# A decoder of two layers: alternating scan steps, and B's rows spread through device memory

## The reference

```python
xs, res = split(rmsnorm(x) @ W_in);  xs = silu(depthwise_causal_conv(xs))
xdbc = xs @ W_xp;  dt_r, B, C = xdbc[:, :128], xdbc[:, 128:144], xdbc[:, 144:160]
delta = softplus(dt_r @ W_dt + b_dt)                     # [256 tokens, 512 channels]
h[t] = exp(delta[t] * A) * h[t-1] + delta[t] * B[t] * u[t]   # 512 channels x 16 states
y = sum over states of h[t] * C[t];   y = (y + u * D) * silu(res);  out = y @ W_out + x
...
y = einsum(silu(g) * u, w_down) for 16 experts, weighted by routing, plus a shared expert
```

## Time and profile before

| | |
|---|---|
| three runs, us | 983.55, 986.10, 978.01 (median 983.55) |
| the profiled execution: its own time, and its span | 984.03 and 982.2 us |
| busy share of the span | PE 89%, DVE 65%, ACT 39%, POOL 37% |
| TensorE's mean granted clock | 0.955 of full |
| first scan step of sequences 0, 1, 2, 3 starts at | 112.6, 315.8, 535.2, 759.5 us |

### The profile page before, as it was taken

One profiled execution on the slowest core, in us unless ns is written; L12 is line 12 of the kernel. 1 busy time (PEld: TensorE's weight loads), 2 busy tenths in 40 slices (PEclk: granted clock), 3 DMA queues, 4 the chain that ended last, 5 costly groups with the idle time before them and its releaser, 6 DMA issues.

```text
span 982.2 us, 13012 instructions
## 1 busy us (share of the span) xinstructions
PE 870.8 (89%) x4643; PEld 652.0 (66%) x4668; DVE 643.3 (65%) x1378; ACT 383.9 (39%) x828; POOL 358.9 (37%) x393
## 2 busy tenths in 40 slices
PE   6897675988999998889999998888999998789997
PEld 5675344754787786744787886653788786426886
DVE  6332799795355998895355999875355999764333
ACT  4111743326236443426326443417226544243111
POOL 5202485120042875220043875220042876000322
PEclk9897877999999999999999999979999999879999
DMA  6204000002023330301024330302022330300452
GB/s 217 110 0 175 0 1 0 1 14 98 1 81 113 126 113 2 107 29 82 1 81 145 97 111 1 108 1 110 1 68 69 94 109 17 108 1 1 129 153 84
DMA packets 22196, 67.69 MB, mean 69 GB/s; under 512 B 2860, under 2 KB 4780, under 8 KB 21492
## 3 DMA queue, kind: packets, MB, share of 16 engines
q1 hardware_dynamic: 21876, 66.80, 20.8%
q10 hardware_dynamic: 256, 0.07, 0.0%
HBM read 65.74 MB, written 1.05 MB: 68 GB/s over the span
## 4 chain that ended last, share of the span: by engine, by line
PE 49%; DVE 19%; POOL 12%; issue 12%; ACT 7%; DMA 1%; ACTq 1%; POOLq 0%; DVEq 0%; SPq 0%
PE B L779 22%; PE F L779 21%; POOL arena L465 7%; DVE arena L1430 5%; DVE nmx L1501 3%; PE B L1068 3%; POOL spare L550 2%; ACT big L746 2%; POOL arena L475 2%; PE F L808 1%; DVE arena L1270 1%; DVE arena L1442 1%; PE F L790 1%; POOL rs L447 1%; PE B L1149 1%
## 5 line engine op out<-in xcount | busy, mean ns | idle before, releaser
L779 PE MATMUL B<-spare,mw 128*128 128x256 f32 x880 | 209.3, 382 | 0.0
L779 PEld LDWEIGHTS B<-spare,mw 128*128 128x128 f32 x880 | 166.5, 191 | 24.8 <-issue 2.6
L550 POOL TENSOR_TENSOR spare<-q_t 128x256 f32<-128x256 f32 x112 | 82.0, 738 | 193.3 <-DVE q_t L1567 134.2
L1430 DVE TENSOR_TENSOR_SCAN arena<-F,arena 128x512 f32<-128x512 f32 x128 | 149.5, 1207 | 3.7 <-ACT F L702 2.3
L465 POOL TENSOR_TENSOR arena<-du,arena 128x1024 f32<-128x1024 f32 x60 | 140.9, 2360 | 9.8 <-PE F L779 8.5
L702 ACT ACTIVATE F<-delta,a_neg 128x255 f32<-128x255 f32 x256 | 109.9, 467 | 72.6 <-DVE arena L1430 72.6
L779 PE MATMUL B<-mw,spare 128*128 128x256 f32 x448 | 115.4, 381 | 1.2 <-POOL spare L550 1.2
L779 PE MATMUL F<-arena,ident 128*128 128x256 f32 x400 | 105.1, 406 | 1.4 <-POOL arena L475 1.0
L768 ACT ACTIVATE q_t<-B 128x256 f32<-128x256 f32 x112 | 42.0, 381 | 159.2 <-PE B L779 152.6
L1562 DVE SCALAR_TENSOR_TENSOR q_t<-q_t,B 128x256 f32<-128x256 f32 x112 | 46.6, 416 | 77.7 <-ACT q_t L768 77.4
L779 PEld LDWEIGHTS B<-mw,spare 128*128 128x128 f32 x448 | 84.2, 190 | 15.9 <-POOL spare L550 3.9
(11 more groups left out here) (228 smaller groups left out, 1284.0 us busy)
## 6 DMA issues: line engine op xcount, KB each, us to landing
mw<-in_w_moe SPq DMA_DIRECT2D x112, 384.0 KB, 3.1
room<-in_w_f SPq DMA_DIRECT2D x4, 2544.0 KB, 9.1
room<-in_w_l SPq DMA_DIRECT2D x4, 768.0 KB, 7.1
w_m<-in_w_m SPq DMA_DIRECT2D x1, 2112.0 KB
room<-in_w_l SPq DMA_DIRECT2D x4, 512.0 KB, 4.9
x_t<-in_x_t SPq DMA_DIRECT2D x4, 256.0 KB, 3.3
x_tok<-in_x_tok SPq DMA_DIRECT2D x4, 256.0 KB, 6.4
y<-x SPq DMA_DIRECT2D x4, 256.0 KB, 2.2
```

Of the source, the lines that this page charges most:

```text
L550: g.tensor_tensor(hid1[0:r, m % HID_RING, :], hraw[0:r, m % 3, :], crs[0:r, int(m >= MTE), :], ALU.mult)\
L779: return t_.matmul(dst, lhsT, rhs, start=start, stop=stop, skip_group_check=True)
L1430: v.tensor_tensor_scan(h, F[i][:, :], h, 0.0, ALU.mult, ALU.add)\
```

## The change

**Scan order.** Step n is now state pair k = n // 2 of channel pair n % 2. The two pairs alternate, so C's pair is spread once for two steps, eight times for a sequence. Each channel pair sums into a bank of its own, the first into F[3], the second into K[2]. Both are gated in u1, and step 9 gates nothing.

**B.** PE and ACT no longer spread B. SP writes the 16 rows of B (16 KB) to a scratch in device memory, waits for it, and then issues eight transfers that read a pair of rows (2 KB) into all 128 partitions of b_rep, 256 KB each. POOL waits for these.

**The experts.** K[2] is taken, so while a front runs beside the back the tiles go through K[0] and K[1] (gate_bank), and PE's tile m waits for DVE's tile m-2 where it waited for m-3. The last back, which runs alone, keeps three banks. SP's request for the weights of tile m+6 stands three phases later in its own order, with the same wait.

**Order.** All four tables are new.

```diff
+        def gate_bank(b, m):
+            return K[m % (3 if b == B - 1 else 2)]
+        def y_bank(dp):
+            return K[2] if dp else F[3]
...
+                if ph == "d1":
+                    sp.wait_ge(*af.at("bct", b))
+                    sp.dma_start(b_out[b], bct[0:NS, :]).then_inc(b_saved, 16)
+                    sp.wait_ge(b_saved, b * 16 + 16)
+                    for k in range(NK):
+                        sp.dma_start(b_rep[:, k, :], b_out[b, 2 * k:2 * k + 2, :].rearrange("s t -> (s t)")
+                                     .partition_broadcast(P)).then_inc(rep_in[k], 16)
...
-                if ph in BE and BE.index(ph) + MW_RING < MT1:
-                    m = BE.index(ph)
+                if ph in BE and 3 <= BE.index(ph) < MT1 - MW_RING + 3:
+                    m = BE.index(ph) - 3
                     sp.wait_ge(*pb.at(f"down{m}", b))
...
-                dp, k = divmod(n, NK)
+                k, dp = divmod(n, 2)
                 if dp == 0:
-                    pool.wait_ge(*af.at(f"rep{k}", b))
+                    pool.wait_ge(rep_in[k], b * 16 + 16)
...
-                if ph == "d3":
-                    replicate(b, 0)
...
-                    for k in (1, 2, 3):
-                        replicate(b, k)
...
-                spread(F[2], NS + 2 * (n % NK), f"c{n}")
+                spread(F[2], NS + n, f"c{n}")
...
-                        last = mm(F[3][:, i * S:i * S + S], ident[:, :], state(n)[:, i, s * S:s * S + S],
+                        last = mm(y_bank(dp)[:, i * S:i * S + S], ident[:, :], state(n)[:, i, s * S:s * S + S],
...
                     n = STEPS.index(ph)
-                    spread_c(b, n)
-                    if n < 2:
-                        for k in (4 + 2 * n, 5 + 2 * n):
-                            replicate(b, k)
+                    if n % 2 == 0:
+                        spread_c(b, n)
...
-                    if m >= 3:
-                        pe.wait_ge(*db.at(f"gu{m - 3}", b))
+                    r = 3 if b == B - 1 else 2
+                    if m >= r:
+                        pe.wait_ge(*db.at(f"gu{m - r}", b))
...
-                    if n == NK + 1:
-                        gated_output(b, 0)
-                    dve.wait_ge(*pf.at(f"c{n}", b))
+                    dve.wait_ge(*pf.at(f"c{n - n % 2}", b))
...
                 if ph == "u1":
+                    gated_output(b, 0)
                     gated_output(b, 1)
...
-AFTER_PE = {"load": 2, "qkv": 1, "at2": 2, "at3": 1, "at4": 2, "at5": 2, "at6": 1, "at7": 7, "oa": 2, "ob": 5, "xa":
-            1, "xb": 1, "xc": 1, "xd": 6, "fa1": 1, "fa2": 1, "fa3": 1, "fg0": 1, "fg1": 1, "fg4": 1, "fg5": 1, "fd1":
-            3, "fd2": 1, "fd3": 2, "m1": 1, "m2": 2, "m3": 1, "d1": 1, "d2": 1, "d3": 1, "d4": 1, "s0": 1, "s1": 1,
-            "s2": 1, "s3": 1, "s4": 1, "s5": 2, "s6": 1, "s7": 2, "s9": 3, "s10": 1, "s11": 1, "s13": 1}
+AFTER_PE = {"load": 2, "qkv": 1, "at1": 1, "at2": 2, "at3": 1, "at4": 2, "at5": 1, "at6": 2, "at7": 3, "oa": 2, "ob":
+            8, "xa": 1, "xb": 1, "xc": 4, "xd": 3, "fa1": 1, "fa2": 1, "fa3": 2, "fg0": 1, "fg2": 1, "fg3": 3, "fd1":
+            1, "fd2": 1, "m1": 4, "m2": 1, "m3": 1, "d3": 1, "d4": 1, "s0": 3, "s3": 1, "s4": 5, "s6": 1, "s7": 1,
+            "s8": 3, "s10": 1, "s11": 2, "s13": 1}
```

74 lines of the change are left out of this document (29 added, 45 removed), and 6 rows, old and new, of the table AFTER_DVE.

## The result

The changed kernel takes **969.47 us** (median of four runs, 968.47 to 971.54), against 980.92 for the kernel before in the same comparison: 0.987 of its time, with a 95% interval of 0.984 to 0.990. Its profiled execution took 970.11 us with a span of 968.3, against 984.03 and 982.2. So there are 13.9 us between the two traces, and the prediction's sum had 12.6.

A forecast was written before the change was run, and what follows sets the result against it. The scan was taken as bound by DVE, with PE close behind. Three rounds of -3.3 - 0.6 + 0.2 (scan's end) - 0.3 = -4.0, plus sequence 0's -0.6, made 984.0 - 12.6 = 971.4, said as 971 us; range 962 to 986.

The forecast's parts named there:

- The chain to the first scan: From the copy of B and C to a round's first scan: -3.3 us a round, bounds -3.4 to -0.5.
- The memory's branch: Ahead of the first scan: B written to device memory and read back, 2.2 + 3.1 us, first product done at 312.0 to 312.2.
- ACT's branch: Ahead of the first scan: softplus, table load, tanh and decays on ACT, giving a first scan at 312.4, 3.4 us earlier.
- rival 1: Ahead of the first scan: write and read take 8 us or more, gain 0.5 not 3.3; about 976 to 984, chance 0.26.
- So I count it at nothing: In the scan: 5.8 us a round of PE's spreads removed, valued at nothing by itself because DVE's 70 us hides it.
- The scan stage, -0.6: In the scan: gating leaving step 9 -1.6, new DVE waits +2.2, present waits gone -1.2, so -0.6 us a round.
- The three new waits: In the scan: DVE waits for tile 16 (0.8 us), C's pair in s6 (0.7) and tile 21 (0.7).
- rival 2: Expert tiles in the scan: two banks make DVE wait, 0.5 us a tile, 8.5 a round; above 984, chance 0.11.
- The rest of the round, -0.3 a round: Outside chain and scan: new tables let shifts take up some idle PE time, -0.3 us a round, bounds -2 and +2.
- rival 3: Row maxima ahead of the scan: TensorE's clock fall in sequence 3 (4.8 us) does not come; below 966, chance 0.16.
- Sequence 0, -0.6: Sequence 0's front: scan starts +1.0 us later waiting for memory, gating leaves (-1.6), 0.2 added behind: -0.6 us.
- a risk for the output projection: Sequence 0's front: with less PE work, last sums and output projection may start at the low clock; one fall adds up to 4.8 us.

The follow-up runs named there:

- experiment 4: Changed kernel, with SP writing B's rows to the scratch four times, each waited for, before the reads: 992.1 us, 1.012.
- experiment 1: Kernel before, with only the order of the scan's front changed (five table places moved from behind d1 or d2 to behind s0): 984.12 us, 1.001.
- experiment 3: Changed kernel, but B spread by PE and copied by ACT again, with no scratch in memory: 974.46 us, 0.992.
- experiment 6: Changed kernel, with two of B's eight reads issued at once and six behind the weights of tiles 12 and 13: 966.48 us, 0.983.
- experiment 7: Changed kernel, with each spread of C's pair made three times, 32 more bf16 matmuls a round in the scan: 973.44 us, 0.991.
- experiment 12: The changed kernel again, unaltered, timed in six more runs: 968.57 us, 0.986.
- experiment 8: Changed kernel, with PE making the scores of row maxima 4 to 15 twice ahead of the scan: 982.29 us, 1.000.
- experiment 9: Changed kernel, with the old table order ahead of the scan's front (load to m5), new tables from d1 on: 982.54 us, 0.999.
- experiment 11: Changed kernel with B's reads in two parts and one PE table entry moved, leaving the instruction order the same as without that move: 966.72 us, 0.982.
- experiment 5: Kernel before, with only two banks for the expert tiles beside a front, PE's tile m waiting for DVE's m-2: 992.1 us, 1.010.
- experiment 10: Kernel before, code unchanged, with the new table order only ahead of the scan's front (load to m5): 979.59 us, 0.996.
- experiment 2: Changed kernel's code with the four tables of the kernel before: 991.9 us, 1.012.

## Why the prediction was right, and where it was not

The total, 971 for 969.5, is right, and its largest term is right for the reasons given. The rest holds luck. Between the two traces the scan stages came out 5.6 us worse than forecast over the three rounds; the rest of the rounds (1.8 better), sequence 0 (1.6), the tail (3.2) and the chains (0.3) made up for that. Of these the tail is outside the sum altogether, and the rest of the rounds gained by a clock that the sum had kept out.

**The chain to the first scan: right.** -3.4 measured for -3.3, 7.23 us after the copy for 7.2. The memory's branch took 4.9 us from the write's issue to POOL's start, for 5.3: the write landed in 1.4 where 2.2 was taken, and a read of 256 KB, in a row of eight, has a median of 5.3 on the page:

```profile
arena<-b_out SPq DMA_DIRECT2D x32, 256.0 KB, 5.3
```

That median is of all eight, which share the engines; the first one is what POOL waits for. It is ACT's branch that the forecast called last, and in the trace it ends within 0.1 us of DVE's own products for tile 10, which wait for ACT's tanh. Experiment 4 shows the other side of it: late by 4.3, the memory's branch is last, as rival 1 said. The Trainium skill's figure ("DMA: Bandwidth & Descriptors", "Anatomy of one DMA"), about 2.0 us of fixed cost for a transfer, is fitted to transfers that GpSimd issues; this write, issued by SyncE, took 1.4 us.

**"So I count it at nothing": the step that failed.** The prediction called the scan bound by DVE, with PE close behind, and gave the spreads removed from PE no value. For the order before, the traces bear out the first half: DVE has 69.0 us of work in 73.7, some 2.7 us in gaps of under 0.15 us between its instructions, and only these waits:

```profile
DVE arena L1442 <- PE F L779: 1.3, 3, 0.6
DVE arena L1430 <- POOL arena L458: 0.4, 1, 0.4
DVE q_t L1562 <- ACT q_t L768: 0.2, 1, 0.2
```

But the same change also moves an expert tile from the chain into the stage, and there PE's work is no longer free. Without the removal of work the chain's gain of 4.1 us is given back in full, most of it in DVE's waits for PE (experiment 1). Putting work back on PE in the new order has a price in both runs that do it: 1.1 us a round for B's spreads (experiment 3 against 6), and 1.8 us for twice the spreads of C that the change took away (experiment 7 against 6, at full clock; 1.3 by the medians). An estimate from these, 1.1 and half of 1.8, is that the removed spreads are worth about 2 us a round. With all of the change and the weights in time (experiment 6) the stage is 4.3 us shorter than in experiment 1; what else is in this, with DVE's 2.3 us less of work the nearest, isn't shown. The size of the work was off as well: 48 matmuls by 8.7 us made 0.18 each. In the changed kernel's trace a pair from 309.89 on is busy for 0.38 us, yet the next matmul starts at 310.11, 0.22 us after it, and one more in a row costs 0.105 (experiment 7), so 32 fewer are 3.4 us of PE a round and not 5.8.

DVE's work went from 69.0 to 67.5 us, and little of that is seen: even in experiment 6 the stage is only 0.3 us shorter than before. DVE's waits are 2.6 us there where they were 1.9.

**The scan stage, -0.6: it was +0.9, +1.8 and +1.1.** The prediction's walk followed DVE, counted 1.6 for the gating that leaves, and called tile 12's late weights covered because DVE takes the tile only near 325. The lateness itself was forecast well (a request at 308.5, PE waiting some 2 us), and a wait of that size is covered: where no half clock follows it the stage is 73.5 (experiment 12). The three new waits that the walk found for DVE are there as well, 0.8, 1.0 and 0.8 us for 0.8, 0.7 and 0.7. What was missed is the half clock that mostly follows, and that on PE the next spread of C stands behind tiles 12 and 13, so DVE meets the delay at 322 and not at 325. In 18 stages (the changed kernel's two traces, experiments 6, 8, 9 and 11) the length is 73.4 us and this one wait of DVE, to within 0.15 us. It is 1.30, 2.15 and 1.51 us in the changed kernel, not there in experiments 6 and 11, and up to 3.40 in experiment 8. So this is 1.2 to 2.0 us a round. Without it the term would have been -0.3, near the forecast.

**Two banks, rival 2.** The mechanism exists: 8.6 us in the old order (experiment 5), just as the rival priced it for one round, over three. In the changed kernel the stage shows no PE wait for a DVE product, as the walk had found; in experiment 6 there is one of 1.6 us, whose cost was not measured. So the new tables hide the two banks in the changed kernel; whether they do once the weights are in time is open.

**The rest of the round, -0.3 a round.** The new order ahead of the scan gives the first two rounds nothing (+0.4 and +1.3 after, +1.1 and +0.2 in experiment 10), and the third 3.7. There the half clock of 10.2 us doesn't come. That is part of rival 3, which the prediction priced at 4.8 and kept out of its sum. It is in experiment 10, where nothing else is changed, and in its median, -4.5.

The rival's reason is not borne out, though. It had the new order prevent the fall of the clock. In the traces with that order (the changed kernel twice, experiments 3, 4, 6, 7, 8, 10 and 11) a fall comes between the scans in 25 of 27 rounds. In those with the old order (before and experiments 1, 2, 5 and 9) it comes in 4 of 15, always in the third round. What is gone is the long one: in the new order each lasts 3.4 or 6.8 us. In the old order it lasts 10.2 us in two traces (before and experiment 1, with 139.9 and 140.0 us between the scans), 3.4 us in experiments 2 and 5, and doesn't come in that of experiment 9, its fastest run.

**Sequence 0, -0.6: it was -2.2.** The scan does wait for POOL there, and POOL for memory, as forecast:

```profile
112.67 2.44 DVE L1419 TENSOR_TENSOR_SCAN arena<-F,arena 128x512 f32<-128x512 f32 x2 [2.47 <-POOL arena L472]
```

but it costs 0.2 and not 1.0. The rest is the gating that leaves step 9: its four operations took 2.4 us of DVE there in sequence 0, not the 1.6 that were counted. Behind the scan DVE waited 2.28 us for PE's last sums before, and the first pair's gating now fills that wait, so the last gating ends 4.5 us after the last scan and not 5.3. The low clock that the Trainium skill's rule ("TensorE: Matmul & The Clock Gate", Part 1) made a risk for the output projection is there in the scan of sequence 0 in both traces (a mean of 0.71 before, 0.75 after), but it is over before the projection: 16 matmuls take 3.72 us after and 3.62 before.

**The tail, -3.2, is not the change's.** The last back's code and order are as they were, but for SP's later requests for weights. Before has 17.1 us at half clock from 850.3 on, after has 3.4 at 854.5; the kernel of experiment 5, whose tail is also untouched, has 145.89 like the changed one, and experiment 7, with the changed kernel's tail, has 149.4 with 20.5 us at half clock. The two medians, which are 11.5 us apart in their own comparison and 14.5 in the later ones, hold such chances too.

## What to carry to other kernels

When two engines are both over 90% busy in a stage, busy shares don't say which owns it. Read the waits of the one taken as the bound: work on the other costs as much as it lengthens those, so test it by adding a known amount of work, and don't price its removal at nothing when the same change brings more work into the stage. Here a tile taken out of a chain landed in the next stage in full until other work had gone from the same engine; code and order have to be judged together (+8 us for the code alone, 0 and -4.5 for the two parts of the order that were run alone, -14.5 together). When an engine is late, follow what stands behind the late work in its own order: here it was not the late tile that DVE met first but the spread of C behind it. A blocking wait in the queue that issues transfers delays whatever is requested behind it: put the two transfers that are needed at once in front, the weights next and the rest last.

## What the runs showed of the hardware

- A write of 16 KB to device memory was confirmed 1.4 us after its issue, and four in a row, each waited for, took 5.7 us. A read of B takes SP 0.43 us to issue and the next starts 0.47 us after it, so eight hold up the next request by 3.7 us.
- After 1.97 us of PE idle ahead of tile 12 the granted clock was 0.50 for 3.4 us; after 7.5 us (experiment 4), for 10.2. But after 2.10 us in experiment 12, 2.50 in experiment 9 and 3.22 in experiment 8 it stayed at 1.00 in one round of each, so the length of the wait alone doesn't say whether the clock falls.
- In the changed kernel's trace the clock falls for 6.8 us in each round ahead of the scan, with PE busy in most of it; here in the second of the three:

```profile
434.70:441.50 6.80, 6.33 (x33) 1.26 (x32) 3.20 (x11) 3.63 (x7) 1.33 (x2) 0.50 0.51 212
```

  In the second trace of the same kernel (experiment 12) the three are 3.4, 6.8 and 6.8 us long. Before, it fell there once in three rounds, for 10.2 us. The runs of the changed kernel differ by 4.5 us, those of the kernel before by 16. That short falls come in every run with the new order, and a long one in some runs with the old, would fit this difference, but the few traces can't show it, and it stays open.
